# A four-layer graph network with a mixture of experts on one core: last tile's rows scattered first, the experts' rows loaded ahead of the table of experts, the tables of picks in the routing buffer

## The reference, cut to what matters

```python
x = _layernorm(x + _L0_gnn_ref(...)); x = _layernorm(x + _L1_gnn_ref(...)); x = _layernorm(x + _L2_gnn_ref(...))
# fourth layer
h = feats * rsqrt(deg_out)[:, None]
m = segment_sum(h[src], dst) * rsqrt(deg_in)[:, None]
x = m @ W_gc + b_gc + (feats @ W_res + b_res)
vals, idx = top_k(x @ Wg + bg, 2); gates = softmax(vals)
...                                             # rows sorted by expert, at most 1024 for each
h1 = gelu(buf @ w1[e] + b1[e])                  # 256 -> 512, exact gelu
h2 = h1 @ w2[e] + b2[e]                         # 512 -> 256
y = x + sum of gates * h2 over both picks
return batchnorm(y) * gamma + beta
x = _layernorm(x + fourth layer)
```

## Time and profile before

| | us |
|---|---|
| median of three runs (2097.65 to 2101.59) | 2098.84 |
| the profiled execution, its own time | 2101.84 |
| its span in the profile | 2099.6 |
| PE busy | 1814.2 (86%) |
| DVE busy | 908.4 (43%) |
| ACT busy | 498.6 (24%) |
| POOL busy | 464.1 (22%) |

### The profile page before, as it was taken

One profiled execution on the slowest core, in us unless ns is written; L12 is line 12 of the kernel. 1 busy time (PEld: TensorE's weight loads), 2 busy tenths in 40 slices (PEclk: granted clock), 3 DMA queues, 4 the chain that ended last, 5 costly groups with the idle time before them and its releaser, 6 DMA issues. The chain is left out here.

```text
span 2099.6 us, 34207 instructions
## 1 busy us (share of the span) xinstructions
PE 1814.2 (86%) x9538; PEld 1437.0 (68%) x9539; DVE 908.4 (43%) x2709; ACT 498.6 (24%) x1301; POOL 464.1 (22%) x824
## 2 busy tenths in 40 slices
PE   1988886799899999989989999989999599999811
PEld 0355555688788878867768878867777489899700
DVE  4877664444434421122221127756666222122167
ACT  0034444322223311111111111111111123322242
POOL 1022222411112100000000002216666532333203
PEclk8999998899989999999999999999999699999955
DMA  4178999999778868866658878868886599999931
GB/s 126 32 242 286 319 324 337 319 321 321 242 244 267 264 198 283 282 212 213 211 189 282 282 260 281 281 222 256 258 252 183 172 369 379 375 382 377 355 125 61
DMA packets 279196, 545.06 MB, mean 260 GB/s; under 512 B 18198, under 2 KB 201024, under 8 KB 275904
## 3 DMA queue, kind: packets, MB, share of 16 engines
q1 hardware_dynamic: 271072, 526.38, 75.9%
q0 software_dynamic: 8032, 17.60, 2.2%
HBM read 415.19 MB, written 128.72 MB: 259 GB/s over the span
## 5 line engine op out<-in xcount | busy, mean ns | idle before, releaser
L1045 PE MATMUL psum<-xsa,blk 128*128 128x512 f32 x2500 | 647.8, 408 | 18.3 <-DVEq L363 8.2
L1045 PEld LDWEIGHTS psum<-xsa,blk 128*128 128x128 f32 x2500 | 462.0, 191 | 113.3 <-issue 11.3
L1045 PE MATMUL psum<-xsb,blk 128*128 128x512 f32 (+1 forms) x1875 | 424.4, 374 | 5.9 <-DVEq L363 5.9
L1045 PEld LDWEIGHTS psum<-xsb,blk 128*128 128x128 f32 x1875 | 324.4, 192 | 69.5 <-issue 7.0
L1810 POOL TENSOR_SCALAR ve<-mv 128x1 f32<-128x1 f32 x75 | 16.9, 225 | 829.7 <-DVE mv L1521 829.7
L1406 DVE TENSOR_SCALAR onehots<-counts_scratch 128x348 bf16<-128x348 f16 x464 | 161.7, 374 | 82.3 <-issue 41.9
L947 PE MATMUL psum<-onehots 128*128 128x349 bf16 x464 | 149.4, 322 | 38.7 <-DVE onehots L1411 38.3
L950 PE MATMUL psum<-zrow 128*128 128x512 bf16 x464 | 176.4, 390 | 0.0
L524 PE MATMUL psum<-route,expert_weights 128*128 128x128 f32 x1360 | 168.3, 277 | 0.0
L524 PEld LDWEIGHTS psum<-route,expert_weights 128*128 128x128 f32 x1360 | 160.4, 194 | 0.3
L534 PE MATMUL psum<-expert_weights,route 128*128 128x256 f32 x672 | 159.1, 380 | 0.3 <-ACT route L581 0.3
(11 more groups left out here) (303 smaller groups left out, 2107.6 us busy)
## 6 DMA issues: line engine op xcount, KB each, us to landing
blk<-counts_src_on_rows SPq DMA_DIRECT2D x125, 832.0 KB
blk<-counts_src_on_rows SPq DMA_DIRECT2D x125, 768.0 KB
expert_weights<-in_L_gnn_w SPq DMA_DIRECT2D x176, 512.0 KB, 5.9
blk<-counts_dst_on_rows SPq DMA_DIRECT2D x50, 832.0 KB
counts_dst_on_rows<-band_rows SPq DMA_DIRECT2D x25, 1600.0 KB, 8.1
blk<-counts_dst_on_rows SPq DMA_DIRECT2D x50, 768.0 KB
counts_src_on_rows<-blk SPq DMA_DIRECT2D x13, 1600.0 KB, 8.6
counts_src_on_rows<-rblk SPq DMA_DIRECT2D x12, 1600.0 KB, 9.7
```

Of the source, the lines that this page charges most:

```text
L1045: mm = e.matmul(o, blk[n][:, k * P:(k + 1) * P], XS[:, k, :, 0:Fw], start=(k == 0), stop=(k == T - 1 and not own))
```

## The change

The two picks' rows of a tile are scattered in `l3_scatter`, the numbers in a new step `l3_ids`, with a semaphore of its own, `ids_scattered`. In POOL's pipeline the order for tiles 0 to 23 is pages, keep, rows, numbers; for tile 24 it is rows, pages, numbers. SP waits for the 50 scatters of rows, loads four chunks of rows, then waits for `experts_known` and for the 50 scatters of numbers, loads the table of picks, and then the four b2. PE transposes the table of picks after the hidden layer of chunk 0, and only its 116 rows; DVE copies it after the rows of chunks 0 and 1. So that rows can be loaded while the routing uses its scratch, `xin` moves to the last 4096 of `route`'s 20,480 bytes, which the scratch leaves free; the tables of picks move from buffers of their own into `route`, ahead of `xin`, and the start of the table of numbers is made in `G`.

```diff
--- before.py
+++ after.py
@@ -179,9 +179,6 @@
         slot_to = sb("slot_to", [P, TOP, T], U32)
 
         pick_id = sb("pick_id", [P, TOP, T])
-        pick_rows = sb("pick_rows", [P, P])
-        pick_of = sb("pick_of", [P, P], U32)
-        pick_col = [sb(f"pick_col{n}", [P, 1], U32) for n in range(RING)]
 
         def view(buf, at, n, dt):
             w = 2 if dt in (F32, I32, U32) else 1
@@ -294,18 +291,29 @@
         beyond, at = cut(mx, at, (1,))
         ecol, at = cut(mx, at, (2,))
         eint, at = cut(mx, at, (2,), I32)
-        assert at <= 10240
+        assert at <= 10240 - 2 * RING * F
 
         w1s, w2s, xin, xTs, hTs, yout, b2s = ([] for _ in range(7))
         for base, lot, room in ((mw, ((w1s, (KF, H), RING), (w2s, (HT, F), RING)), T * PARTS * F * 2),
-                                (mx, ((xin, (F,), RING), (yout, (F,), RING), (b2s, (F,), RING), (xTs, (F,), 2),
-                                      (hTs, (HT, P), 2)), 10240)):
+                                (mx, ((yout, (F,), RING), (b2s, (F,), RING), (xTs, (F,), 2), (hTs, (HT, P), 2),
+                                      (xin, (F,), RING)), 10240)):
             at = 0
             for bufs, shape, n in lot:
                 for _ in range(n):
+                    if bufs is xin and n == RING and not bufs:
+
+                        at = 10240 - 2 * RING * F
+                        rows_at = at
                     v, at = cut(base, at, shape)
                     bufs.append(v)
             assert at <= room
+
+        at = 2 * F * (2 * RING + 2) + 2 * 2 * HT * P
+        pick_rows, at = cut(mx, at, (P,))
+        pick_of, at = cut(mx, at, (P,), U32)
+        pick_cols, at = cut(mx, at, (RING,), U32)
+        pick_col = [pick_cols[:, n:n + 1] for n in range(RING)]
+        assert at <= rows_at
         picked_rows = mw[:, :].bitcast(F32).rearrange("p (t k f) -> p t k f", t=T, k=TOP)
         at = 0
         sums_of, at = cut(mx, at, (T // SPLIT, F))
@@ -456,11 +464,13 @@
             for c in range(RING):
                 load_w1(c, c)
                 load_w2(c, c)
+            e.wait_ge(S("rows_scattered"), 16 * TOP * T)
+            for c in range(RING):
+                load_rows(c, c)
             e.wait_ge(S("experts_known"), 1)
-            e.wait_ge(S("rows_scattered"), 2 * 16 * TOP * T)
+            e.wait_ge(S("ids_scattered"), 16 * TOP * T)
             e.dma_start(pick_rows[0:NCH, :], ids[0:NCH * P, :].rearrange("(c p) a -> c (p a)", p=P)).then_inc(S("inputs_loaded"), 16)
             for c in range(RING):
-                load_rows(c, c)
                 load_b2(c, c)
             turns = e.value_load(nturn[0:1, 0:1], min_val=1, max_val=MAXCH // RING)
             with e.Fori(0, turns) as j:
@@ -536,11 +546,11 @@
                 mm.then_inc(S("chunk_summed"), 1)
 
             turns = e.value_load(nturn[0:1, 0:1], min_val=1, max_val=MAXCH // RING)
-            e.wait_ge(S("inputs_loaded"), 16 * (LOADS + 2))
-            e.transpose(psum[:, 6, 0:P], pick_rows[:, :], identF[:, :]).then_inc(S("ids_turned"), 1)
             turn(0, 0, 0, 0)
             turn(1, 0, 1, 1)
             hidden(0, 0, 0, 0)
+            e.wait_ge(S("inputs_loaded"), 16 * (LOADS + 2))
+            e.transpose(psum[:, 6, 0:NCH], pick_rows[0:NCH, :], identF[0:NCH, 0:NCH]).then_inc(S("ids_turned"), 1)
             with e.Fori(0, turns) as j:
                 for n in range(RING):
                     c = RING * j + n
@@ -638,11 +648,11 @@
                 e.wait_ge(S("chunk_turned"), c + 1)
                 e.tensor_copy(xTs[par], psum[:, par, 0:F]).then_inc(S("chunk_copied"), 1)
 
-            e.wait_ge(S("ids_turned"), 1)
-            e.tensor_copy(pick_of[:, :], psum[:, 6, 0:P]).then_inc(S("picks_known"), 1)
             e.sem_inc(S("chunk_made"), 2)
             copy_turned(0, 0)
             copy_turned(1, 1)
+            e.wait_ge(S("ids_turned"), 1)
+            e.tensor_copy(pick_of[:, 0:NCH], psum[:, 6, 0:NCH]).then_inc(S("picks_known"), 1)
             turns = e.value_load(nturn[0:1, 0:1], min_val=1, max_val=MAXCH // RING)
             with e.Fori(0, turns) as j:
                 for n in range(RING):
@@ -802,7 +812,7 @@
 
             phase_end(e, "load")
             phase_end(e, "table")
-            e.dma_start(ids[0:NCH * P, :].rearrange("(p c) a -> p (c a)", p=P), pick_rows[:, 0:NCH])\
+            e.dma_start(ids[0:NCH * P, :].rearrange("(p c) a -> p (c a)", p=P), G[:, 0:NCH])\
                 .then_inc(ld, 16)
             assert n[0] == 16 * LOADS
             e.wait_ge(ld, 16 * (LOADS + 1))
@@ -1756,7 +1766,7 @@
             e.iota(pick_id[:, :, :], [[1, TOP], [TOP * P, T]], base=0, channel_multiplier=TOP,
                    allow_small_or_imprecise_dtypes=True).then_inc(S("masks_set"), 1)
 
-            e.iota(pick_rows[:, :], [[1, P]], base=TOP * NP, channel_multiplier=NCH,
+            e.iota(G[:, 0:P], [[1, P]], base=TOP * NP, channel_multiplier=NCH,
                    allow_small_or_imprecise_dtypes=True).then_inc(S("masks_set"), 1)
             e.iota(pcol[:, :], [[0, 1]], base=0, channel_multiplier=1, allow_small_or_imprecise_dtypes=True)\
                 .then_inc(S("masks_set"), 1)
@@ -1835,8 +1845,11 @@
                 for k in range(TOP):
                     e.indirect_dma_start(out=xbuf, out_offset=bass.IndirectOffsetOnAxis(ap=slot_to[:, k, i:i + 1], axis=0),
                                          in_=X4[:, i, :], in_offset=None).then_inc(S("rows_scattered"), 16)
+
+            def l3_ids(i, par):
+                for k in range(TOP):
                     e.indirect_dma_start(out=ids, out_offset=bass.IndirectOffsetOnAxis(ap=slot_to[:, k, i:i + 1], axis=0),
-                                         in_=pick_id[:, k, i:i + 1], in_offset=None).then_inc(S("rows_scattered"), 16)
+                                         in_=pick_id[:, k, i:i + 1], in_offset=None).then_inc(S("ids_scattered"), 16)
 
             def l3_pages(i, par):
 
@@ -1853,7 +1866,15 @@
                 e.tensor_tensor(rooms[:, 0, :], rooms[:, 0, :], grown, ALU.add).then_inc(done, 1)
                 e.wait_ge(done, PAGE_STEPS * (i + 1))
             e.wait_ge(S("pages_set"), 1)
-            pipeline(e, [(2, l3_pages), (1, l3_keep), (2, l3_scatter)], unrolled=True)
+            def l3_first(i, par):
+                if i < T - 1:
+                    l3_pages(i, par)
+
+            def l3_last(i, par):
+
+                if i == T - 1:
+                    l3_pages(i, par)
+            pipeline(e, [(2, l3_first), (1, l3_keep), (2, l3_scatter), (2, l3_last), (2, l3_ids)], unrolled=True)
             e.wait_ge(S("tile_x4_kept"), past("l3", "x4_kept") + T)
             pool_moe(e)
```

## The result

| | before | after |
|---|---|---|
| median, us | 2098.84 (2096.67 to 2107.87, 5 runs) | 2085.48 (2084.10 to 2086.38, 5 runs) |
| profiled execution, us | 2101.84 | 2085.62 |
| its span, us | 2099.6 | 2083.4 |

The ratio of the runs is 0.9913, with a 95% interval of 0.9884 to 0.9943: under 2%, but the interval leaves out 1. Lines of the changed kernel are 8 to 13 higher: L1055 is the aggregation product, L1726 the slots, L666 the output of a chunk, L553 the transpose of picks.

The account below looks back on a forecast made before the run. The passage from the last tile's routing to the first expert output was taken as bound by the wait for scattered numbers; first output 4.3 us earlier, passed on to the end, gave 2098.84 - 4.3 = 2094.5 us, range 2092.0 to 2097.5.

Parts of the forecast that it names:

- the paragraph on the rest: Small side effects: transpose, copy and table edits under 0.1 us, hidden under PE; lower buffer addresses taken as nothing, +-1 us.
- The claim that the table of picks becomes the bound: Before the first output: the numbers land at 1653.4, PE's transpose of picks follows at 1656.7, and this hardly moved chain bounds.
- A hole of 1.7 us: PE idles between first hidden layer, ending 1655.0, and transpose of picks at 1656.7; the clock's count begins anew.
- the 23.3 us of the forecast: DVE's first output of a chunk comes at 1662.8 to 1663.7, a gain of 3.9 to 4.8, middle 4.3 us.
- The rows' landing: Last tile's second scatter of rows, issued at 1641.65, lands 5.3 us later, at 1647.0; 7.3 kept for a rival.
- The 1646: Estimate of when the last tile's rows are in, by the Trainium skill's fixed part of about 2.0 us.
- The third of my signs of being wrong: Wrong if the distance from the first output of a chunk to the end changes by more than 1 us.
- The second: Wrong if SP's wait for the numbers, ahead of loading the table of picks, ends later than 1654.
- the warm one: Rival: rows land after 7.3 us, PE stays without a hole, clock rises earlier; gain 5.5, 2093.3 us; chance 0.25.
- the numbers are worked off one after the other: Rival: the last tile's scatters of numbers queue, landing at 1654.6, 1.2 later; gain 3.1, 2095.7 us; chance 0.15.
- The clock did not stay low into the turns of the loop: Slower rival: PE's holes keep the clock at 0.50 into the loop's first turns; 2099 to 2103 us; chance 0.05.
- No gain: Rival: the experts' stretch, full on PE and DMA, gives the gain back in added stalls; 2098 us; chance 0.07.

Follow-up runs that it names:

- e1: Kernel before, order unchanged, only the tables of picks moved to the far end of SBUF, so buffers behind begin 1152 bytes lower; 2089.37 us, ratio 0.995.
- e7: Changed kernel with the last two steps of POOL's pipeline swapped for the last tile: numbers right behind rows, pages last; 2082.24 us, ratio 0.9914.
- e9: Changed kernel with 24 products of zeros on PE where it waits for the table of picks; 2082.47 us in one run.
- e10: Changed kernel without the scatter of numbers of the last tile's second pick, SP waiting for one fewer; 2083.65 us in one run.
- e12: Changed kernel with picks transposed behind chunk 1 and the four b2 loaded ahead of SP's wait for the numbers; 2087.69 us, ratio 0.9918.
- e13: Changed kernel with picks transposed behind chunk 1 and the four b2 loaded with the first weights, into buffers no longer needed; 2080.41 us, ratio 0.9887.
- e5: Changed kernel with an unused buffer of 64 bytes ahead of the features' parts; 2092.10 us in one run.
- e2: Changed kernel with an unused buffer of 1152 bytes where the tables of picks lay, restoring the addresses of before; 2095.54 us, ratio 0.9979.
- e3: Changed kernel with an unused buffer of 128 bytes ahead of the features' parts; 2094.97 us in one run.
- e11: Changed kernel scattering 128 pieces of 512 bytes instead of the 4-byte numbers, picks not told; 2080.16 us in one run.

## Why the prediction was wrong

**The term that failed** is the one in the paragraph on the rest: "Buffers behind the removed tables begin about 1 KB lower; no row prices that, and I take nothing, bounds +-1 us". Both halves failed. It was worth 14.5 us ahead of the passage in this pair of profiles (12.7 in e1, which has the addresses alone; some 1.5 of the 14.5 is the low clock that only the kernel before had), and probably the 1.6 us the other way behind it. The first removes 3.5 ns on the mean (15.2 us over 4375; 5 ns where PE runs nothing else) from each of the products that carry half the span; a bound of 1 us asks that they move by no more than 0.23 ns on the mean, and nothing in the profile gave that. What the runs show in its place is that the distance between the weights and the moving operand, modulo 256 bytes, sets the rate of these products: it was 128 and became 0. That this made the kernel faster is luck; by the same rule the removal would have cost as much in a layout where the distance was 0 before. The chain of waits gave 21% of the span to these products, and I never asked what the edit does to them, for I read only the passage that the order of the work touches.

The passage, step by step (times behind the slots' end, 1639.94 before and 1625.41 after):

| step | predicted | measured |
|---|---|---|
| second scatter of rows starts | 1.7 | 1.6 |
| rows landed | 7.1 | 4.0 |
| first hidden layer ends | 15.1 | 11.4 |
| numbers landed | 13.5 | 14.0 |
| transpose of picks | 16.8 | 17.7 |
| idle time of PE before it | 1.7 | 6.3 |
| clock rises, behind the transpose | 4.2 to 5.9 | 3.4 |
| first output of a chunk | 23.3 | 23.7 |

The claim that the table of picks becomes the bound was right. The next hidden layer did run low, but by another hole than the predicted one: 6.3 us and not 1.7. A hole of 1.7 us would hardly have done it, for the clock stayed at 1.00 through 2.9 us of the real one, and in e7, with a hole of 0.34, it did not fall at all. So the 23.3 us of the forecast are partly luck: rows that landed 3 us too early for it opened the hole that made its low clock true.

The rows' landing was mis-sized: I took 5.3 us from a scatter at the end of the experts, under full load, where 2.4 was true in a quiet queue. The Trainium skill's 2.0 us (page "DMA: Bandwidth & Descriptors", section "Anatomy of one DMA") was nearer, and the trace agrees with it for rows; it is far off for the numbers, 8.0. The 1646 that the prediction made of that figure was a wrong sum as well: 1641.65 + 2.0 is about 1643.7, an estimate, and the measured landing, 4.0 us behind the slots, is about 1644 on the same axis. The error in the rows did not move the forecast, since they were not the bound; it hid that PE would idle long enough to lose the clock, 1.7 us by e9.

The third of my signs of being wrong came true: from the first output to the end it took 432.1 us before and 434.3 after, 2.3 us more and not within 1. The second, SP's wait for the numbers ending later than 1654, lies on its edge: 14.1 us behind the slots, which is 1654.0.

Of the rivals, the warm one (rows land late) did not happen in the changed kernel, and did in e7, with its gain. That the numbers are worked off one after the other was refuted by e10; what lengthens their lag is loads beside them (e12 against e13, and probably e7). The clock did not stay low into the turns of the loop. "No gain" was right in one point: the experts' stretch gave back 1.6 us, though probably by an address and not by added load.

## What to carry to other kernels

Ask of every buffer that an edit removes, adds or resizes what it does to the addresses behind it: a change of 0.2% in order came with 0.5% in addresses. Where one engine spends most of the span on one instruction, put the start-to-start time of that instruction, in a stretch where PE runs nothing else, beside the same figure of the next version. A table of small numbers that is scattered by DMA and read at once is dear; keep it off the path and keep loads away from it.

## What the runs showed of the hardware

- Products of 128x128 blocks with 128x512 features in fp32, at a granted clock of 1.00: 227 ns from start to start where weights and moving operand lie a multiple of 256 bytes apart (fourteen traces), 229 at 64 off (e5), 232 at 128 off (before, e2, e3).
- A scatter of 128 numbers of 4 bytes landed 7.3 to 8.4 us after its issue where no load was issued behind it, 10.4 beside loads of rows (e7), 15.8 beside loads of b2 (e12); one of 128 pieces of 512 bytes 2.3 us (e11), one of 1 KB 2.4 us.
- The granted clock of PE stayed at 1.00 for 2.9 us of a hole of 6.3 us and then fell to 0.50. In the changed kernel it rose 4.2 and 3.4 us after work was taken up, in e9, e11 and e13 6.1 to 6.5 us after.
- Loads of experts' weights beside full DMA traffic (1700 to 1900 us) landed 5.5 to 5.8 us after their issue, on the median, where the weights' buffers begin at a multiple of 256 bytes, and 6.0 to 6.2 us where they do not.
